# The masked decay rows of the back stage: one broadcast multiplication on POOL in place of eight scalings on ACT

## The reference, cut to what matters

```
decay = exp(dt * A)                    # dt: softplus, [b, L, 8 heads]
h = h * decay + (dt * xh) outer B      # one step for each of the 512 times
y = h . C + D_skip * xh
u = rms(y * silu(z)) @ out_proj
```

## Time and profile before

| | us |
|---|---|
| median of three runs | 1590.02 |
| profiled execution | 1586.75 |
| its span, first to last instruction | 1585.0 |
| PE busy | 1401.9 (88%) |
| ACT busy | 1113.8 (70%) |
| DVE busy | 1064.8 (67%) |
| POOL busy | 63.3 (4%) |

### The profile page before, as it was taken

One profiled execution on the slowest core, in us unless ns is written; L12 is line 12 of the kernel. 1 busy time (PEld: TensorE's weight loads), 2 busy tenths in 40 slices (PEclk: granted clock), 3 DMA queues, 4 the chain that ended last, 5 costly groups with the idle time before them and its releaser, 6 DMA issues.

```text
span 1585.0 us, 35918 instructions
## 1 busy us (share of the span) xinstructions
PE 1401.9 (88%) x13330; PEld 1023.4 (65%) x13330; DVE 1064.8 (67%) x2383; ACT 1113.8 (70%) x3382; POOL 63.3 (4%) x118
## 2 busy tenths in 40 slices
PE   6899899998899889999988899998889999889666
PEld 5788666665567556677666667766666776666444
DVE  3666666665678778778777777777777777777101
ACT  3555688885678887777787777777877777787221
POOL 1100000001000000000000000000000000000000
PEclk9999899998999999999999999999999999999655
DMA  8222310002221112112101211210121121010000
GB/s 272 82 94 93 101 52 1 1 1 71 63 81 55 54 29 85 63 41 81 54 28 55 81 41 42 81 55 28 55 81 42 47 77 53 28 55 2 7 20 27
DMA packets 69596, 90.42 MB, mean 57 GB/s; under 512 B 5488, under 2 KB 58736, under 8 KB 69040
## 3 DMA queue, kind: packets, MB, share of 16 engines
q1 hardware_dynamic: 69312, 87.87, 17.4%
q0 software_dynamic: 112, 0.26, 0.1%
HBM read 71.33 MB, written 16.78 MB: 56 GB/s over the span
## 4 chain that ended last, share of the span: by engine, by line
PE 60%; ACT 19%; DVE 11%; issue 9%; DMA 1%; POOL 0%; ACTq 0%; DVEq 0%; POOLq 0%; SPq 0%
PE ps L1156 14%; PE ps L1424 10%; PE ps L1450 8%; PE ps L1163 8%; PE ps L1170 6%; DVE arena L1105 4%; PE ps L1409 3%; PE ps L1489 3%; ACT arena L686 3%; ACT dAm L544 2%; PE ps L1229 2%; PE ps L1280 2%; ACT arena L693 2%; ACT L655 1%; ACT R L745 1%
## 5 line engine op out<-in xcount | busy, mean ns | idle before, releaser
L1156 PE MATMUL ps<-W,arena 128*128 128x128 f32 x2896 | 428.9, 282 | 28.7 <-ACT arena L686 18.1
L1156 PEld LDWEIGHTS ps<-W,arena 128*128 128x128 f32 x2896 | 328.5, 147 | 175.4 <-issue 129.2
L686 ACT ACTIVATE arena<-ps,nmax 128x512 f32<-128x512 f32 x640 | 434.4, 685 | 2.3 <-DVE nmax L1085 1.6
L693 ACT COPY arena<-ps 128x512 f32<-128x512 f32 x320 | 187.0, 584 | 209.1 <-PE ps L1156 204.9
L1085 DVE TENSOR_REDUCE nmax<-ps 128x1 f32<-128x512 f32 x320 | 206.1, 685 | 120.2 <-PE ps L1424 81.5
L1105 DVE COPY arena<-ps 128x512 f32<-128x512 f32 x320 | 213.7, 686 | 23.5 <-PE ps L1156 10.1
L1424 PE MATMUL ps<-W,arena 32*128 32x512 f32 x1280 | 182.8, 638 | 35.1 <-DVE arena L1105 34.8
L1450 PE MATMUL ps<-arena 128*32 128x128 f32 x5120 | 173.0, 276 | 32.0 <-ACT arena L693 31.7
L1088 DVE TENSOR_REDUCE nmax<-ps 128x2 f32<-128x1024 f32 x160 | 193.7, 1211 | 0.0
L1450 PEld LDWEIGHTS ps<-arena 128*32 128x32 f32 x5120 | 130.0, 109 | 69.4 <-ACT arena L693 59.3
L1409 PEld LDWEIGHTS ps<-R,at 128*128 128x128 f32 x768 | 115.1, 189 | 47.8 <-DVE R L1068 26.5
(11 more groups left out here) (210 smaller groups left out, 1726.1 us busy)
## 6 DMA issues: line engine op xcount, KB each, us to landing
W<-keys SPq DMA_DIRECT2D x48, 512.0 KB, 3.6
arena<-values SPq DMA_DIRECT2D x48, 512.0 KB, 4.8
keys<-W SPq DMA_DIRECT2D x16, 448.0 KB, 3.3
values<-W SPq DMA_DIRECT2D x16, 448.0 KB, 3.9
W<-keys SPq DMA_DIRECT2D x16, 256.0 KB, 2.8
arena<-values SPq DMA_DIRECT2D x16, 256.0 KB, 3.3
W<-in_pack SPq DMA_DIRECT2D x1, 3180.0 KB, 10.1
W<-in_pack SPq DMA_DIRECT2D x1, 2246.0 KB, 10.6
```

The lines of the kernel that those rows point to most:

```text
L686: nc.scalar.activation(Pr[:, a, :], ps[:, a, :], ACT.Exp, bias=nmax[:, u % 32:u % 32 + 1], accum_out=den[:, u % 32:u % 32 + 1]).then_inc(s ...
L693: nc.scalar.copy(PT[:, (4 * Q + a) % 8, :, :].rearrange("p k n -> p (k n)"), psT).then_inc(sem("u_ev_act"), 1)
L1156: ins = nc.tensor.transpose(dst[:, k * P:(k + 1) * P], src[:, k * P:(k + 1) * P], ident)
```

## The change

The eight activations of `masked_dA` leave ACT's list. POOL does one tensor_tensor instead, with both operands broadcast: the mask over the heads and the column of dA over the 128 columns. For tile 0 POOL waits for `m_soft` and for the parameters (`par1`), and for tile k+1 it waits for `m_rows` = 2k+1, which says that PE has read dAm of tile k, ahead of `root` for tile k. ACT no longer waits for `m_soft` = 19. `m_dAm` counts once a tile as before, and PE's list and DVE's are the same.

```diff
--- before.py
+++ after.py
@@ -427,7 +427,17 @@
                 if k == 4:
                     pool.wait_ge(sem("mod_mm"), 1)
                     pool.memset(Hst[:, :, :], 0.0).then_inc(sem("zeroed"), 1)
+            def masked_dA(k):
+                nc.gpsimd.tensor_tensor(dAm[:, :, :], w("tri_le").unsqueeze(1).to_broadcast([P, HM, P]),
+                                        wide(dts[:, 11, k, :], P), ALU.mult).then_inc(sem("m_dAm"), 1)
+
+            pool.wait_ge(sem("m_soft"), 19)
+            pool.wait_ge(sem("par1"), 16)
+            masked_dA(0)
             for k in range(NT):
+                if k + 1 < NT:
+                    pool.wait_ge(sem("m_rows"), 2 * k + 1)
+                    masked_dA(k + 1)
                 root(rooms[k % 2].st[:, 2:3], rooms[k % 2].st[:, 1:2], "m2", k + 1)
 
             pool.wait_ge(sem("m_x1"), NT)
@@ -539,13 +549,6 @@
                     nc.scalar.activation(dts[:, 3, :, :], dts[:, 2, :, :], ACT.Exp).then_inc(sem("m_exp"), 1)
                     nc.scalar.activation(negA[:, :], w("alog"), ACT.Exp).then_inc(sem("m_exp"), 1)
 
-            def masked_dA(k):
-                for h in range(HM):
-                    ins = nc.scalar.activation(dAm[:, h, :], w("tri_le"), ACT.Identity, scale=dts[:, 11, k, h:h + 1])
-                ins.then_inc(sem("m_dAm"), 1)
-
-            act.wait_ge(sem("m_soft"), 19)
-            masked_dA(0)
             keep_item(NT - 1, 1)
             silu(NT - 1, 0)
             silu(NT - 1, 1)
@@ -586,8 +589,6 @@
                         ins = nc.scalar.activation(r.xw[:, h * HP:(h + 1) * HP], r.xdt[:, h * HP:(h + 1) * HP], ACT.Identity,
                                                    scale=r.dec[:, 1, h:h + 1])
                     ins.then_inc(sem("m_xw"), 1)
-                    if k + 1 < NT:
-                        masked_dA(k + 1)
                     act.wait_ge(sem("m_y3"), k + 1)
                     nc.scalar.activation(r.y2, r.y, ACT.Square, accum_out=r.st[:, 0:1]).then_inc(sem("m2_ss"), 1)
```

## The result

The changed kernel has a median of 1580.86 us over 20 runs (1577.33 to 1589.11), the kernel before 1590.05 over 20 (1587.39 to 1594.18): ratio 0.9943, 95% interval 0.9931 to 0.9955, so 9.2 us or 0.57% less. Forecast were 1580.5 us and 9.5 us less.

What follows compares the result with a forecast made beforehand. In the back stage PE is busiest, but ACT's L544 closes each tile and PE waits for dAm. Terms -9.8 (14 intervals), -1.5 (first interval) and +1.8 (start) give -9.5 us, a median of 1580.5 us, range 1574 to 1588.

Steps and rivals of the forecast that it cites:

- The tile: Back stage, one tile: L1280 follows L1316 sooner without L544 ahead of it, 0.7 us less, from 11.58 to 10.87 us.
- The 14 intervals: Back stage, L1280 of tile 1 to that of tile 15: 14 x 0.7 = 9.8 us less.
- rival C: POOL's operation gets ahead of L950 in every tile and holds it; tile 13.37 us, some 1615 us in all; chance 0.09.
- The first interval: Behind tile 0: L1280 goes sooner after L1316, 1.5 us less, bounds 1.3 and 1.57.
- The start: Convolution L842 ahead of tile 0: its second operation is held by POOL's, 2.55 us, less 0.76 of waiting; +1.8 us.
- POOL's operation: The multiplication of 128x1024 added on POOL in each tile takes 2.55 us, weighed between 2.0 and 2.9.
- L955 starting when one ends: Sign that the forecast is right: in each tile DVE's L955 is held, 0.64 us, until POOL's operation ends.
- The cover: In a tile, POOL's operation is free up to about 3.3 us; the tile pays what exceeds it.
- The sum: Whole kernel: -9.8 - 1.5 + 1.8 = -9.5 us, for a median of 1580.5 us.
- Everything behind the back stage shifts as a whole: The attention behind the back stage, 1185 us, holds nothing the diff touches and only moves in time.
- The shared access: SBUF: a DVE operation with two SBUF operands is held until POOL's is done; one reading one SBUF operand, L953, passes.
- Rivals B, D and E: B: POOL operation 4 us; D: 5.8 us; E: PE pauses before L1280 for another reason; B and E 0.10, D 0.03.

Runs made afterwards that it cites:

- third experiment: The changed kernel, with POOL's multiplication also waiting for m_un so that it can't come ahead of L951; 1574.29 us, ratio 0.9899 to the kernel before.

## Why the attention stage varies

In the attention stage PE's clock falls at some places and not at others. One fall of the changed kernel, in stretches of 4 us:

```profile
1111.60:1115.60 4.00, 3.24 (x27) 2.14 (x25) 3.06 (x8) 3.94 (x10) 0.00 (x0) 1.00 0.00 0
1115.60:1119.60 4.00, 3.02 (x42) 2.51 (x43) 2.49 (x7) 3.78 (x12) 0.00 (x0) 0.81 0.00 0
1119.60:1123.60 4.00, 4.00 (x27) 3.10 (x25) 3.11 (x11) 1.66 (x6) 0.55 (x1) 0.77 0.01 2
```

0.81 and 0.77 over 4 us each are 1.7 us at full clock lost. Set side by side by POOL's root operations, the attention stages of two profiles run in step and part in jumps of about 1.7 us at such places. From 40 us behind the start of the stage to 110 us before its end, what the lower clock takes (time by the share of the clock that is missing) is:

| profiled execution | lost there | from 20 us before the stage to 40 us behind its start | UT memset to the fifth root behind it |
|---|---|---|---|
| before | 1.7 | 6.8 | 86.8 |
| before, once more | 8.5 | 6.8 | 87.5 |
| changed | 13.7 | 8.5 | 88.6 |
| changed, once more | 6.8 | 8.5 | 88.5 |
| third experiment | 8.5 | 5.1 | 87.3 |
| third, once more | 8.5 | 5.1 | 87.1 |

The first column varies for one and the same kernel, so most of the 10.7 us between the first two profiles, 12.0 by this column, are such falls. The other two columns repeat: where the back stage goes over into the attention stage, the changed kernel loses more to the lower clock than the kernel before, both times, and the third experiment less, and the fifth root comes 1.1 to 1.8 us later than before. In both profiles of each kernel it is the same, so it looks to belong to the kernel and not to chance. The executions point the same way: the mean granted clock is 0.9543 in 33 of the kernel before, 0.9520 in the 26 of the changed kernel and 0.9555 in the 12 of the third experiment, each known to some 0.0007. What in a kernel decides this no run shows.

## Why the prediction was right, point by point

- **The tile.** Forecast 0.7 us less, measured 0.82 (11.58 to 10.76). From the start of L1316 to that of L1280 it takes 0.91 us in place of 1.62, which is the 0.7; and the first weight load now lies under L1317, so L1281 takes 1.88 us in place of 1.98. The chain was right: PE lacked this much, and half of ACT's work could go back for nothing.
- **The 14 intervals.** Forecast 9.8 us, measured 9.9 (162.08 to 152.20): 11.5 by the tile, less 1.6 for the one tile in which rival C came true. Two errors that cancel.
- **The first interval.** Forecast 1.5 for the way from L1316 to L1280. It takes 0.97 us in place of 2.43, so 1.46, and the same in the second pair of profiles. From the first exponential on, the first pair has 1.75 us less (11.48 to 9.73).
- **The start.** Forecast +1.8, measured +0.67. This is the term that was mis-sized. Of its two parts (2.55 us for which the convolution is held, less the 0.76 us that L842 no longer waits for ACT) the second came as forecast. The first was 1.51. POOL's operation lasts 1.90 us and not 2.55, which makes 0.65 of the difference; the rest is that POOL's work began, and the convolution then went on, each some 0.2 us sooner than forecast.
- **POOL's operation.** Forecast 2.55 us, measured 2.09, of which 0.2 are L951's hold. The lower of the values weighed, 2.0 for two reads at 0.82 ns and 0.12 us fixed, comes to 1.8 when it is worked out; the measured 1.90 lies between. Whether broadcast operands cost anything can't be told, as no run has the multiplication without them; at 1.90 us they can't cost much. Since the operation is short, L956 isn't held in the steady tile, where 0.64 us were forecast. The sign "L955 starting when one ends" came true by coincidence.
- **The cover.** Forecast: POOL's work is free up to 3.3 us, and the tile pays what exceeds it. With 3.87 us the tile was 0.39 us longer, so it was free up to 3.5.
- **The end of the stage** is 0.6 us shorter, most of it since the last turn still finds the full clock (L1157 takes 0.65 us, before 1.12); it wasn't in the sum.
- **The sum.** Forecast -9.5 us; the back stage gave -11.5 and -11.1 in the two pairs, the medians -9.2. So the sum was 2 us too small for the stage that it describes, and that the total was hit to 0.4 us is luck. "Everything behind the back stage shifts as a whole" wasn't so: the changed kernel's executions are some 2 us longer outside the back stage. At the start of the attention stage 1.1 to 1.8 us of this are seen, at a lower clock; no step of the prediction had it.
- **The shared access.** A DVE operation that meets POOL's is held if it is L951, a tensor_scalar with one tensor operand in SBUF (2.11 us in place of 0.49), or if it has two (L843, 2.27 in place of 0.75; L956, 2.82 in place of 1.22); L954, with one operand in PSUM, passed, as forecast. The Trainium skill, "SBUF — State Buffer", section "Who interferes with whom", says that a DVE instruction with two SBUF inputs contends with a GpSimd instruction that reads SBUF; the 2.27 and 2.82 us agree. It names tensor_scalar among the operations that can take the shared access too; the 2.11 us agree. POOL's operation is held in the same way when it comes second, and its row begins before it gets on. At the start it ends at 188.18 us; 1.90 us of work put its beginning at 186.28, 0.14 us before the convolution's first operation ended (186.43). In the steady tile and in tile 1 the same sum gives 0.14 again, and for the held DVE operations 0.14 to 0.21. So but for these 0.14 to 0.21 us the one that is held waits for the whole of the other.
- **Rival C.** Its margin of 0.23 us was 0.15, and a late start of DVE of 0.35 us was enough to lose it. Its price of 1.8 us a tile was 1.4 to 1.6 at full clock, 3.1 when the clock fell. The prediction's "the order of issue decides who blocks" doesn't hold for the order in which the rows begin: in the tile near 282 us POOL's begins first, and it is POOL that is held.
- Rivals B, D and E fell: POOL's operation is short, and the idle time before L1280 is gone.

## What to carry to other kernels

When work leaves the engine that closes a loop, read how late the next engine is: the gain was 0.8 us a tile, not 2.3. When it goes to POOL, look at which DVE operations lie in the same stretch; a margin of 0.15 us is no order, and a wait that fixes the order (here for `m_un`) costs nothing: it gives 1.6 us in the tile that had lost the race, 2.3 to 2.4 in the stage and 6 in the total, of which the last part isn't explained. Compare stages, not totals, where a later stage varies by more than the change.

## What the runs showed that was not expected

- A POOL multiplication of 128x1024 with both operands broadcast takes 1.90 us alone, 1.86 ns an element; the additions of 128x256 had let 2.4 to 2.8 ns an element expect.
- A pause of PE of 1.5 us in the back stage was followed by a fall of the clock in three tiles of 14, and not in the others of equal length.
